# Row norms, affine step, SiLU and residual addition moved into the aggregate of a graph layer, tile by tile

## The reference, cut to what matters

```
def _gnn_layer(x, row, col, W, b, g, beta):
    agg = segment_sum(x[col], row, num_segments=n)
    deg = maximum(segment_sum(ones, row), 1.0)[:, None]
    h = (x + agg / deg) @ W.T + b
    mu = mean(h, axis=-1, keepdims=True)
    var = mean(square(h - mu), axis=-1, keepdims=True)
    hn = (h - mu) * rsqrt(var + EPS) * g + beta
    return silu(hn)
x1 = _gnn_layer(xn, ..., W0, b0, g0, beta0)
x2 = _gnn_layer(x1, ..., W1, b1, g1, beta1)
x = x + x2 + mix(xn)
```

## Time and profile before

| | us |
|---|---|
| median of three runs | 4776.59 (4770.77 to 4787.19) |
| the profiled execution | 4744.46 |
| its span, first to last instruction | 4742.8 |
| TensorE busy | 3298.2 (70%) |
| VectorE busy | 2080.1 (44%) |
| ScalarE busy | 620.1 (13%) |
| GpSimd busy | 1075.0 (23%) |
| mean granted TensorE clock | 0.818 |

### The profile page before, as it was taken

How to read it: one execution, slowest core, us unless ns; L and a number is a source line. 1 busy time by engine, 2 the same in 40 slices (tenths; PEclk the granted TensorE clock), 3 DMA queues, 4 the chain that set the end, 5 groups by cost and what they waited for, 6 DMA issues and landing times. The chain is left out here.

```text
span 4742.8 us, 52284 instructions
## 1 busy us (share of the span) xinstructions
PE 3298.2 (70%) x14322; PEld 2412.2 (51%) x14323; DVE 2080.1 (44%) x4400; ACT 620.1 (13%) x1234; POOL 1075.0 (23%) x1246
## 2 busy tenths in 40 slices
PE   1899799679846317999549603267777777737998
PEld 0666588568725215777424303144555554525555
DVE  6999601310143630000132284366666666742333
ACT  0111100110022102232102100000000000002222
POOL 2300100000010231000310001666666666400000
PEclk9999899889978658999769856577777776757999
DMA  3522244234300012112223102344444444200000
GB/s 102 218 95 95 100 125 125 69 116 133 97 10 0 0 55 77 49 53 82 62 90 145 62 0 43 102 113 120 119 123 120 120 120 119 71 31 20 14 13 27
DMA packets 311385, 383.64 MB, mean 81 GB/s; under 512 B 42672, under 2 KB 255489, under 8 KB 307841
## 3 DMA queue, kind: packets, MB, share of 16 engines
q1 hardware_dynamic: 240642, 221.16, 14.3%
q0 software_dynamic: 49040, 140.22, 10.3%
q10 hardware_dynamic: 21616, 21.21, 1.5%
HBM read 270.97 MB, written 111.53 MB: 81 GB/s over the span
## 5 line engine op out<-in xcount | busy, mean ns | idle before, releaser
L1972 POOL DMA_INDIRECT att_ring<-relation_rows,table_row x784 | 780.0, 995 | 441.1 <-issue 221.8
L2083 PE MATMUL att_acc<-att_ring,att_onehot 128*128 128x264 f32 x1568 | 529.5, 466 | 214.0 <-issue 196.6
L2083 PEld LDWEIGHTS att_acc<-att_ring,att_onehot 128*128 128x128 f32 x1568 | 340.4, 227 | 353.4 <-issue 302.4
L446 PE MATMUL counts_acc<-onehot_lo,onehot_key 128*128 128x400 bf16 x2000 | 361.7, 336 | 44.6 <-DVE onehot_key L428 44.6
L425 DVE TENSOR_SCALAR onehot_lo<-node_ids,source_lo 128x800 bf16<-128x800 int16 x1000 | 350.9, 419 | 0.0
L446 PEld LDWEIGHTS counts_acc<-onehot_lo,onehot_key 128*128 128x128 bf16 x2000 | 267.8, 139 | 142.6 <-DVE onehot_key L428 84.3
L625 PE MATMUL agg_agg<-x_gnn,agg_slab 128*128 128x257 f32 x1250 | 278.6, 382 | 66.1 <-DMA agg_slab<-edge_counts 66.1
L2046 PE MATMUL att_po<-att_near,att_onehotT 128*128 128x64 f32 x1568 | 229.9, 305 | 94.8 <-DVE att_onehotT L2143 51.8
L625 PE MATMUL agg_agg<-xn,agg_slab 128*128 128x257 f32 x1250 | 277.5, 381 | 22.3 <-DMA agg_slab<-edge_counts 22.3
L625 PEld LDWEIGHTS agg_agg<-x_gnn,agg_slab 128*128 128x128 f32 x1250 | 238.6, 191 | 102.3 <-DMA agg_slab<-edge_counts 66.5
L2046 PEld LDWEIGHTS att_po<-att_near,att_onehotT 128*128 128x128 f32 x1568 | 216.5, 219 | 103.9 <-issue 103.0
(11 more groups left out here) (391 smaller groups left out, 4355.0 us busy)
## 6 DMA issues: line engine op xcount, KB each, us to landing
agg_slab<-edge_counts SPq DMA_DIRECT2D x50, 1600.0 KB, 7.4
edge_counts<-counts_out SPq DMA_DIRECT2D x100, 400.0 KB, 2.4
relation_rows<-tab_out SPq DMA_DIRECT2D x25, 1056.0 KB, 4.0
att_targets<-targets SPq DMA_DIRECT2D x28, 896.0 KB
wide_w<-L_ffn_W ACTq DMA_DIRECT2D x14, 1024.0 KB, 6.9
att_ring<-relation_rows,table_row POOLq DMA_INDIRECT x784
expert_rows_in<-blank_rows POOLq DMA_DIRECT2D x34, 256.0 KB
expert_rows_out<-blank_rows POOLq DMA_DIRECT2D x33, 256.0 KB
```

Source lines behind the costliest of these rows:

```text
L446: mm = nc.tensor.matmul(acc[:, k, h, 0:HALF_LO], oh_key[:, k, :, j], oh_lo[:, k, j, h * HALF_LO:(h + 1) * HALF_LO], start=False, stop=Fals ...
L1972: nc.gpsimd.indirect_dma_start(slots(p)[:, j, :], None, rows_of, bass.IndirectOffsetOnAxis(ap=c.row[:, n:n + 1], axis=0)).then_inc(landed[ ...
L2083: mm = nc.tensor.matmul(acc[:, 0:RW], oh[:, j, :], slots(p)[:, j, :], start=j == 0, stop=False)
```

## The change

Each `aggregate` now does the whole layer. Its `output` adds the bias into a two-buffer tile `h`, takes the row statistics of that tile, works out mean and variance on single columns, waits for a square root from ScalarE, and applies normalization, gain and shift. ScalarE does square root and SiLU of tile t between the copies of tiles t and t+1; in the second aggregate GpSimd adds the result to the residual. The two `normalize` calls and the large `h` are gone.

```
     output(t, b) on VectorE:
+        link = chain(v, norm_s, t * 11)
+        hb, s, f = h[:, b, :], stats[:, b, :], few[:, b, :]
         v.wait_ge(projected, t + 3)
-        nc.vector.tensor_tensor(tile_of(h, t), po[:, b, 0:D], bias[:, :], ALU.add).then_inc(written, 1)
+        v.wait_ge(out_s, t + 1)
+        ins = nc.vector.tensor_tensor(hb, po[:, b, 0:D], bias[:, :], ALU.add)
+        ins.then_inc(written, 1)
+        v.wait_ge(written, t + 3)
+        link(nc.vector.bn_stats(s, hb))
+        link(nc.vector.tensor_tensor(f[:, 0:1], s[:, 1:2], s[:, 4:5], ALU.add))
+        link(nc.vector.tensor_tensor(f[:, 1:2], s[:, 1:2], s[:, 4:5], ALU.subtract))
+        link(nc.vector.tensor_scalar(f[:, 0:1], f[:, 0:1], 0.5, None, ALU.mult))
+        link(nc.vector.scalar_tensor_tensor(out=f[:, 2:3], in0=f[:, 1:2], scalar=D / 4.0, in1=f[:, 1:2], ...))
+        link(nc.vector.tensor_tensor(f[:, 3:4], s[:, 2:3], s[:, 5:6], ALU.add))
+        link(nc.vector.tensor_tensor(f[:, 2:3], f[:, 2:3], f[:, 3:4], ALU.add))
+        nc.vector.tensor_scalar(f[:, 4:5], f[:, 2:3], 1.0 / D, EPS, ALU.mult, ALU.add).then_inc(var_s, 1)
+        v.wait_ge(root_s, t + 1)
+        link(nc.vector.reciprocal(f[:, 3:4], f[:, 5:6]))
+        link(nc.vector.tensor_scalar(hb, hb, f[:, 0:1], f[:, 3:4], ALU.subtract, ALU.mult))
+        link(nc.vector.tensor_tensor(hb, hb, gain[:, :], ALU.mult))
+        link(nc.vector.tensor_tensor(hb, hb, shift[:, :], ALU.add))
+        v.sem_inc(ready, 1)
     ScalarE (step is the copy of before):
-        tiles(act, NT, step)
+        def root(t, b):
+            act.wait_ge(var_s, t + 1)
+            nc.scalar.activation(few[:, b, 5:6], few[:, b, 4:5], ACT.Sqrt).then_inc(root_s, 1)
+        def silu(t, b):
+            act.wait_ge(ready, t + 1)
+            if add_to is None:
+                nc.scalar.activation(tile_of(dst, t), h[:, b, :], ACT.Silu).then_inc(out_s, 1)
+            else:
+                act.wait_ge(added, t + 1)
+                nc.scalar.activation(z[:, b, :], h[:, b, :], ACT.Silu).then_inc(out_s, 1)
+        step(0, 0)
+        with act.Fori(0, NT // 2) as i:
+            root(i * 2, 0)
+            silu(i * 2, 0)
+            step(i * 2 + 1, 1)
+            root(i * 2 + 1, 1)
+            silu(i * 2 + 1, 1)
+            step(i * 2 + 2, 0)
+        root(NT - 1, 0)
+        silu(NT - 1, 0)
     GpSimd, where add_to is given:
+        pl.sem_inc(added, 2)
+        def step(t, b):
+            pl.wait_ge(out_s, t + 3)
+            nc.gpsimd.tensor_tensor(tile_of(add_to, t), tile_of(add_to, t), z[:, b, :], ALU.add).then_inc(added, 1)
+        tiles(pl, NT, step)
     the stage:
-        aggregate(g, "agg0", c, counts, c.xn, w[0], vec[0][0], h)
-        normalize(g, "gn0", c, h, x1, vec[0][1], vec[0][2], silu=True)
-        aggregate(g, "agg1", c, counts, x1, w[1], vec[1][0], h)
-        normalize(g, "gn1", c, h, None, vec[1][1], vec[1][2], silu=True, add_to=c.x)
+        aggregate(g, "agg0", c, counts, c.xn, w[0], *vec[0], dst=x1)
+        aggregate(g, "agg1", c, counts, x1, w[1], *vec[1], add_to=c.x)
```

More of the change, by code:

```diff
@@ L588, in _, with aggregate @@
                     tiles(pl, NT, step)
-def aggregate(g, name, c, counts, xn, wt, bias, h):
+def aggregate(g, name, c, counts, xn, wt, bias, gain, shift, dst=None, add_to=None):
     nc = g.nc
@@ L602, in aggregate @@
         po = g.ps(ctx, f"{name}_out", [P, 2, MMN])
+        h = g.sb(ctx, f"{name}_h", [P, 2, D])
+        z = g.sb(ctx, f"{name}_z", [P, 2, D])
+        stats = g.sb(ctx, f"{name}_stats", [P, 2, 6])
+        few = g.sb(ctx, f"{name}_few", [P, 2, 6])
         loads = [g.sem(f"{name}_load{b}") for b in range(2)]
-        agg, staged, turned, copied, projected, written, link_s = (
-            g.sem(f"{name}_{x}") for x in ("agg", "stg", "trn", "cpy", "prj", "wrt", "chn"))
+        agg, staged, turned, copied, projected, written, link_s, norm_s, var_s, root_s, ready, out_s, added = (
+            g.sem(f"{name}_{x}") for x in ("agg", "stg", "trn", "cpy", "prj", "wrt", "chn", "nchn", "var", "root",
+                                           "affine", "silu", "added"))
         with nc.Block() as block:
@@ L665, in output @@
                 def output(t, b):
+                    link = chain(v, norm_s, t * 11)
+                    hb, s, f = h[:, b, :], stats[:, b, :], few[:, b, :]
                     v.wait_ge(projected, t + 3)
-                    nc.vector.tensor_tensor(tile_of(h, t), po[:, b, 0:D], bias[:, :],
-                                            ALU.add).then_inc(written, 1)
+                    v.wait_ge(out_s, t + 1)
[6 more added lines that the diff above has]
+                    link(nc.vector.tensor_scalar(f[:, 0:1], f[:, 0:1], 0.5, None, ALU.mult))
+                    link(nc.vector.scalar_tensor_tensor(out=f[:, 2:3], in0=f[:, 1:2], scalar=D / 4.0, in1=f[:, 1:2],
+                                                        op0=ALU.mult, op1=ALU.mult))
+                    link(nc.vector.tensor_tensor(f[:, 3:4], s[:, 2:3], s[:, 5:6], ALU.add))
[7 more added lines that the diff above has]
+                    v.sem_inc(ready, 1)
                 mean(0, 0)
@@ L679, in _ @@
                 act.sem_inc(copied, 2)
+                act.sem_inc(out_s, 2)
                 def step(t, b):
@@ L684, in step, with _ @@
                     nc.scalar.copy(stT[:, b, :], pt[:, b, 0:D]).then_inc(copied, 1)
-                tiles(act, NT, step)
+                def root(t, b):
[18 more added lines that the diff above has]
+                silu(NT - 1, 0)
+            if add_to is not None:
+                @block.gpsimd
+                def _(pl):
+                    pl.sem_inc(added, 2)
+                    def step(t, b):
+                        pl.wait_ge(out_s, t + 3)
+                        nc.gpsimd.tensor_tensor(tile_of(add_to, t), tile_of(add_to, t), z[:, b, :], ALU.add
+                                                ).then_inc(added, 1)
+                    tiles(pl, NT, step)
 def turn(g, name, c, src, dst=None, hidden=None, project=None, scalar_stages=False):
@@ L2678, in build_program @@
             with ExitStack() as own:
-                h = g.sb(own, "h_gnn", [P, NT, D])
                 x1 = g.sb(own, "x1_gnn", [P, NT, D + 1])
```

## The result

The changed kernel takes 4664.64 us (median of 4 runs, 4651.46 to 4676.29) against 4774.26 us (4770.77 to 4787.19), a ratio of 0.9762 with a 95% interval of 0.9733 to 0.979. The forecast was 4677, its range 4657 to 4700.

What follows compares the result with a forecast made beforehand. TensorE was taken to bound the aggregate loops, with the normalization stretches after them exposed; gains of 45.6 us (layer 1) and 53.9 us (layer 2), 99.5 us in all, off the 4776.59 us median gave 4677 us, range 4657 to 4700.

Steps and rivals of the forecast that it cites:

- What bounds the stretch: Both aggregates: TensorE bounds the loops, 95% busy; after each, some 60 us of normalization leave it without work.
- the second rival: Warmer TensorE restart and table loads hidden everywhere: gain about 109 us, 4668 us; chance 0.13.
- The restart: First 100 matmuls after each idle stretch: a shorter gap might gain 0 to 2.8 us at each restart; taken 0.
- The steps of the chain: Each tile's bias add, statistics, single-column operations, square root, reciprocal, three passes and SiLU: 7.5 us, in layer 2 6.1.
- The in-loop square root's load: ScalarE's table load before each in-loop square root, taken as exposed behind the wait: 1.43 us from release to start.
- The last tile's chain: Tile after each loop: both activations' table loads hidden, 7.5 - 2 x 1.4 = 4.7 us.
- The last projection: Last tile of each layer: projection may run at 1.2 GHz, 1.1 us each; taken 0.
- The sums: Both layer ends, two chains one after the other: gain 45.6 us in layer 1, 53.9 in layer 2, together 99.5.
- the first rival: Dearer serial chains at the ends, hops and single-column operations twice as long: gain about 84 us, 4693 us; chance 0.16.
- Cover: In the loops, the 7.5 us chain fits in 11.05 us beside the product, 3.5 us to spare; loop costs nothing.
- The slower rival: Late copy idles TensorE in each tile and its clock falls: 83 us over, 4859 us; chance 0.03.
- The baseline: Whole kernel: gain taken off the median of the runs, 4776.59 us, not the profiled execution's 4744.46 us.

Runs made afterwards that it cites:

- Each layer alone: Two kernels, only layer 1 or only layer 2 as in the changed kernel, the other as before: 4535.60 and 4527.49 us, 0.9878 and 0.9863 of the kernel before.
- Root by counter: Changed kernel with the square root's result in a column addressed by the loop counter, not one of two fixed columns: 4677.23 us.
- Nine passes: Changed kernel with nine more linked VectorE passes over 128x256 in each tile's chain: 4504.97 us, 0.9816 of the kernel before.
- eighteen: Changed kernel with eighteen more linked VectorE passes over 128x256 in each tile's chain: 4630.01 us, 1.0083 of the kernel before.
- group 2: Runs on one chip of the kernel before (4772.16 us), the changed kernel again (4669.49 us) and three variants of it.
- group 3: Later runs on another chip: kernel before (4743.36 us), changed kernel (4636.75 us) and two variants of the changed kernel.

## Why the prediction was right, and where it wasn't

**What bounds the stretch** held: TensorE in the loops, the normalization between them. Each layer alone gave its own part, and no product became longer.

**By the time alone** the second rival (4668 us) was nearer than the forecast: 4664.64 lies 12 us under 4677 and just below the forecast's own 4665 to 4690. Its two causes decide. The restart wasn't warm: the first 100 matmuls of layer 2 take 24.36, 24.71 and 24.84 us in the three profiles of the changed kernel against 24.88 and 24.93 before, so 0 to 0.5 us of the 2.8. Of the loads, the square root's were hidden and those of layer 1's SiLU were not. Most of the 12 us came from stages that neither the forecast nor the rival spoke of (7.2 and 2.1 us in the first profiles).

**The steps of the chain** held to 0.03 us: bias add 0.46, statistics 0.46 (forecast 0.49), seven single-column operations at 0.19 (forecast 0.20), three passes at 0.45 to 0.46.

**The in-loop square root's load** was the step that was wrong. I had it behind the wait, 1.4 us in every chain, because the only in-loop load in the trace with a single wait stood there. In the groups of ScalarE's lines after (busy us, mean ns, idle us before and what ended it) the 50 loads ahead of the square root have 0.9 us of idle time before them in all, as have those of layer 2's SiLU 0.4, and only the 25 of layer 1's SiLU (L719) wait:

```profile
L714 ACT ACT_TABLE_LOAD x50 | 64.2, 1283 | 0.9
L719 ACT ACT_TABLE_LOAD x25 | 32.1, 1283 | 41.6 <-DVEq L692 41.6
L722 ACT ACT_TABLE_LOAD x25 | 32.1, 1283 | 0.4
```

The load in the trace of before stood behind its wait for another reason: that SiLU writes a tile addressed by the loop counter. The square root writes a fixed column, and its load ran ahead. The chain was therefore 5.91 us in layer 1 (forecast 7.5) and 4.54 in layer 2 (6.1). The last tile's chain, 4.55 (forecast 4.7), had all its loads hidden as forecast. Root by counter brought back 7.38 us, near the forecast's 7.5.

**The last projection** at the lower clock was in the forecast as a bound of 1.1 us and taken as 0. It cost 0.95 in each layer (2.08 against 1.13), and made up for part of the load's 1.4. That two missed terms went opposite ways, 2.8 us of loads hidden at the ends and 1.9 us of projections, and left 0.9, is luck.

**The sums.** Measured from bias add of tile 23: layer 1 ends its last SiLU after 12.88 us (906.04 to 918.92), forecast 13.8; layer 2 its GpSimd addition after 12.30 (1246.52 to 1258.82), forecast 13.2. The bias add of tile 23 also came 0.4 and 0.7 us earlier after its layer's first matmul, and the time from the last result to the next first matmul was 0.2 and 0.3 us shorter, all within what the loops and ends vary. In all 101.2 to 103.1 us, forecast 99.5. In the forecast itself the first rival's gain of 84 us lies under the 88 that the range is said to start from; nothing hangs on it.

**Cover.** The forecast of 3.5 us to spare was 5.2 in layer 1 because of the shorter chain, and 6.6 in layer 2. Nine passes used 4.1 of it at no price; eighteen went past it and cost what the excess makes. The Trainium skill's drain of 1380 ns with each load ("ScalarE: Activation LUTs", "What ACT_TABLE_LOAD costs") shows nowhere: in the changed kernel the load at 884.74 is followed by its SiLU at 886.03, and a copy that ends at 911.85 + 0.35 by a load at 912.22.

**The slower rival** was rightly small, and also wrong in its price. With eighteen more passes, TensorE's idle time in each tile does come with a lower granted clock (0.94 and 0.97), but this adds nearly nothing while the chain sets the pace.

**What the forecast left out** is the 6.4 to 7.2 us of the second mix stage and the 2 to 3 us of the stages ahead of it, which no row of the changed stage could have told. The medians give 102.7 us (group 2), 106.6 (group 3) and 109.6 (first runs), so the forecast was short by 3 to 10.

**The baseline.** I took the gain off the median of the timed runs and not off the profiled execution, and that came out right: the profile of the kernel before has the attention stage's 1163 us of group 3, and the timed runs, at 4771 to 4787 us, are like group 2's 4768 to 4789. No profile of the kernel before exists from such an occasion, so this last step is inferred.

## What to carry to other kernels

Row work that stands between two TensorE-bound loops can go inside the loop before it, for as long as its chain is shorter than the product that runs beside it: measure the idle time in front of the instruction that ends up queued behind the chain, here the copy, and that is the budget. What can't be hidden is the last tiles, so look at the order of their instructions apart from the loop's: an instruction that another engine waits for should not stand behind work that nobody waits for yet. When two profiles disagree with two medians, compare stage by stage before explaining a number: between the first two profiles a stage with no edit in it hid a third of the gain. And before a difference of 1 or 2 us is given a cause, look at what two profiles of one and the same kernel differ by.

## What the runs showed of the hardware that I had not expected

- A table load of 1.28 us runs ahead of its activation's wait when the activation's operands are at fixed addresses, and behind the wait when one of them is addressed by the loop counter: square root at a fixed column, load 0.02 us behind the copy (892.08); the same square root writing by counter, load 0.11 us after the variance (706.70). With two waits it still stands behind one of them (1322.59 and 1813.84 in the kernel before).
- An untouched loop of 200 statistics instructions took 58.7, 57.6 or 52.7 us, depending on the kernel around it and the same within 0.1 us each time that kernel ran.
- The same attention stage took some 1004, 1165 or 1190 us on three occasions, each on another chip, in groups of kernels that differed by 2 to 7 us among themselves.
- Four matmuls of the projection took 2.08 us after 6.04 or 4.67 us without work for TensorE, at a granted clock of 0.50 in the first case, and 1.13 us after 0.53 us at 1.00.
